# A loop over periods on five engines, written out with constant waits

## The reference

```python
h = tok(x)                        # deformable sampling: 32x32 grid of queries, 8 points each
h = concatenate([h, txt], axis=1) # 1024 + 128 = 1152 tokens of 64 channels
h = h + attention(layernorm(h))   # causal, one head, 64 wide
h = h + ffn(layernorm(h))         # 16 experts, top 2, relu, 64 -> 128 -> 64, then layer norm
```

## Time and profile before

| | us |
|---|---|
| median of 3 runs | 4752.04 |
| lowest, highest | 4744.88, 4759.59 |
| the profiled execution | 4752.51 |
| its span | 4750.7 |
| PE busy | 3648.8 (77%) |
| POOL busy | 3313.9 (70%) |
| DVE busy | 3015.8 (63%) |
| ACT busy | 2167.0 (46%) |

### The profile page before, as it was taken

The page is one execution under the profiler, slowest core; times in us unless marked ns, Lnnn a source line. Parts: engine busy times, 40 slices in busy tenths (PEclk is TensorE's granted clock), DMA queues, the critical chain, the costliest instruction groups (busy, mean ns, idle before and its releaser), DMA issues.

```text
span 4750.7 us, 94109 instructions
## 1 busy us (share of the span) xinstructions
PE 3648.8 (77%) x24896; PEld 3139.7 (66%) x24896; DVE 3015.8 (63%) x9660; ACT 2167.0 (46%) x5266; POOL 3313.9 (70%) x3217
## 2 busy tenths in 40 slices
PE   4686887878778777877878887887878788788842
PEld 2565766767667676766767676775767677676732
DVE  1485858576684857767575775858577585767512
ACT  2354554444445444444544454454454445444401
POOL 0776777777677767777677776767777776777353
PEclk9888888888889888888988888898888978888855
DMA  7759584865848477584857758485774848562422
GB/s 238 247 154 273 160 266 132 253 190 181 244 126 267 131 234 218 164 256 119 258 146 238 222 161 246 125 262 148 221 237 141 259 125 267 151 177 58 120 66 62
DMA packets 922887, 895.94 MB, mean 189 GB/s; under 512 B 123866, under 2 KB 804442, under 8 KB 922200
## 3 DMA queue, kind: packets, MB, share of 16 engines
q1 hardware_dynamic: 785800, 577.28, 40.6%
q0 software_dynamic: 136528, 312.25, 22.0%
HBM read 562.75 MB, written 328.03 MB: 188 GB/s over the span
## 4 chain that ended last, share of the span: by engine, by line
PE 26%; issue 16%; DVE 16%; POOL 16%; DMA 9%; SPq 8%; ACT 7%; DVEq 1%; ACTq 0%; POOLq 0%
POOL ya L785 7%; POOL gath L753 7%; PE ps L862 4%; DMA xg<-xs_d 3%; PE ps L1005 3%; PE ps L876 3%; PE ps L1013 3%; POOL xs_d L769 3%; PE ps L807 2%; SPq L672 2%; PE ps L937 2%; SPq L699 2%; SPq L706 2%; DMA fm<-in_x 2%; SPq L700 1%
## 5 line engine op out<-in xcount | busy, mean ns | idle before, releaser
L753 POOL DMA_INDIRECT gath<-table,idx x2048 | 2107.0, 1029 | 885.9 <-issue 625.9
L785 POOL DMA_INDIRECT ya<-ys_d,row x576 | 585.5, 1017 | 343.5 <-issue 170.3
L1215 DVE TENSOR_TENSOR prod<-gath,corner_w 128x1024 f32<-128x1024 f32 x512 | 622.7, 1220 | 313.9 <-PE ps L862 186.9
L862 PE MATMUL ps<-const,prod 128*128 128x128 f32 x4096 | 628.3, 304 | 229.8 <-DVE prod L1215 211.8
L769 POOL DMA_INDIRECT xs_d<-xm,row x576 | 611.8, 1062 | 189.3 <-issue 173.2
L862 PEld LDWEIGHTS ps<-const,prod 128*128 128x128 f32 x4096 | 541.6, 159 | 265.9 <-issue 174.3
L876 PE MATMUL ps<-w_kv,samp_t 128*128 128x128 f32 x4096 | 634.4, 305 | 7.4 <-ACT kv_sb L1029 6.7
L876 PEld LDWEIGHTS ps<-w_kv,samp_t 128*128 128x128 f32 x4096 | 588.6, 219 | 68.5 <-issue 52.6
L959 PEld LDWEIGHTS ps<-v_sb,probs_t 128*128 128x128 f32 x2880 | 402.4, 212 | 165.7 <-DVE h L1223 75.8
L959 PE MATMUL ps<-v_sb,probs_t 128*128 128x64 f32 x2880 | 423.1, 293 | 112.6 <-DVE h L1223 69.5
L1029 ACT ACTIVATE rows<-ps 128x512 f32<-128x512 f32 x512 | 305.2, 596 | 428.5 <-PE ps L807 424.9
(11 more groups left out here) (162 smaller groups left out, 6156.4 us busy)
## 6 DMA issues: line engine op xcount, KB each, us to landing
table<-rows SPq DMA_DIRECT2D x224, 1024.0 KB
fm<-in_x SPq DMA_DIRECT2D x256, 512.0 KB
wx<-w_d SPq DMA_DIRECT2D x832, 128.0 KB
gath<-table,idx POOLq DMA_INDIRECT x2048
table<-rows SPq DMA_DIRECT2D x32, 960.0 KB
xg<-xs_d SPq DMA_DIRECT2D x208, 130.0 KB
ys_d<-yx SPq DMA_DIRECT2D x208, 128.0 KB
xs_d<-xm,row POOLq DMA_INDIRECT x576
```

Source lines behind the costliest of these rows:

```text
L753: pool.indirect_dma_start(out=gath[:, n % NG, p, :], out_offset=None, in_=tables[par], in_offset=bass.IndirectOffsetOnAxis(ap=idx[:, par, ...
L785: pool.indirect_dma_start(out=ya[:, k, t, :], out_offset=None, in_=ys_d[par], in_offset=bass.IndirectOffsetOnAxis(ap=row[:, par, n:n + 1], ...
L862: last = pe.matmul(bank(0, p * P, p * P + P), prod[h][:, (p * 2 + dx) * P:(p * 2 + dx + 1) * P], ident, is_transpose=True, start=(dx == 0) ...
L1215: return dve.tensor_tensor(o, a, b, op)
```

## The change

`Pair` loses the loop's variable and is always a plain number; `drive` writes periods 0 to 14 one after the other; `settle` waits for a constant. Nothing in TURNS or LAST changes, and no tile, DMA or operation is added, moved or dropped. The counters that kept DVE's steps in line with the loop go.

```diff
-    def __init__(self, off, eng=None, turn=None):
-        self.off, self.eng, self.turn, self.products = off, eng, turn, {}
+    def __init__(self, off):
+        self.off = off
...
     def times(self, per, k=0):
 
-        if self.turn is None:
-            return self.off * per + k
-        if per not in self.products:
-            self.products[per] = self.eng.snap(self.turn * (2 * per))
-        return self.products[per] + (self.off * per + k)
+        return self.off * per + k
...
-            for k in range(LOOP_FROM):
+            for k in range(PAIRS - 1):
                 stretch(1 + k, None)
                 follow(engine, stages, k, Pair(k), k % 2)
-            with eng.Fori(0, (LOOP_TO - LOOP_FROM) // 2) as j:
-                for par in range(2):
-                    pair = Pair(LOOP_FROM + par, eng, j)
-                    stretch(LOOP, pair)
-                    follow(engine, stages, LOOP_FROM + par, pair, par)
-            for k in range(LOOP_TO, PAIRS - 1):
-                stretch(LOOP + 1 + k - LOOP_TO, None)
-                follow(engine, stages, k, Pair(k), k % 2)
-            stretch(LOOP + PAIRS - LOOP_TO, None)
+            stretch(PAIRS, None)
             follow_last(engine, stages)
...
             def settle():
 
-                n = marks.get(thread[0], start[0])
-                if before[0] is None:
-                    dve.wait_ge(vec, n)
-                else:
-                    pair, head = before[0]
-                    dve.wait_ge(vec, pair.times(STEPS[LOOP], head + n))
+                dve.wait_ge(vec, marks.get(thread[0], start[0]))
```

More of the change, by code:

```diff
@@ L231 @@
 FIRST_PART = 3
-LOOP_FROM, LOOP_TO = 2, PAIRS - 2
-LOOP = 1 + LOOP_FROM
 TURNS = {
@@ L324 @@
 class Pair:
-    def __init__(self, off, eng=None, turn=None):
-        self.off, self.eng, self.turn, self.products = off, eng, turn, {}
+    def __init__(self, off):
+        self.off = off
     def __add__(self, n):
-        p = Pair(self.off + n, self.eng, self.turn)
-        p.products = self.products
-        return p
+        return Pair(self.off + n)
     def __sub__(self, n):
@@ L580, in drive @@
                     stages[stage](Pair(0), 0, *args)
-            for k in range(LOOP_FROM):
+            for k in range(PAIRS - 1):
                 stretch(1 + k, None)
                 follow(engine, stages, k, Pair(k), k % 2)
-            with eng.Fori(0, (LOOP_TO - LOOP_FROM) // 2) as j:
-                for par in range(2):
-                    pair = Pair(LOOP_FROM + par, eng, j)
-                    stretch(LOOP, pair)
-                    follow(engine, stages, LOOP_FROM + par, pair, par)
-            for k in range(LOOP_TO, PAIRS - 1):
-                stretch(LOOP + 1 + k - LOOP_TO, None)
-                follow(engine, stages, k, Pair(k), k % 2)
-            stretch(LOOP + PAIRS - LOOP_TO, None)
+            stretch(PAIRS, None)
             follow_last(engine, stages)
-            stretch(LOOP + 1 + PAIRS - LOOP_TO, None)
+            stretch(PAIRS + 1, None)
         def first_of(pair):
-            return pair.turn is None and pair.off == 0
+            return pair.off == 0
         def begun(pair):
-            return pair.turn is not None or pair.off >= 0
+            return pair.off >= 0
         def unseen(n, pair):
@@ L1177, in _ @@
             marks = {}
-            before = [None]
             def step(ins):
@@ L1636, in _ @@
                    const[:, GY:GY + QT_N].unsqueeze(2).to_broadcast([P, QT_N, 2 * NP_]), ALU.add))
-            done = [None, 0]
             def stretch(n, pair):
-                last, count = done
                 assert not any(g.begun for g in staged), [g.begun for g in staged if g.begun]
[L1645 to L1655, removed]
                 start[0] = steps[0]
                 marks.clear()
-            setup_steps = steps[0]
             drive(dve, "vector", {"off_hidden": parts(off_hidden), "off_gelu": parts(off_gelu), "off_points": parts(off_points),
@@ L1666, in _ @@
                         "finish": parts(finish)}, stretch)
-STEPS = (34, 242, 334, 404, 404, 602)
 def kernel(**inputs):
```

## The result

The changed kernel takes 4708.69 us (median of six runs, 4705.71 to 4721.56), the kernel before 4755.82 us (six runs, 4744.88 to 4770.92). The ratio is 0.9905, with a 95% interval of 0.9889 to 0.9921: the change wins 45 us, 38 to 53. I had forecast 10. A second comparison, in another batch of runs, gave 0.9877 (0.9858 to 0.9896), 59 us of 4763.18.

The account below looks back on a forecast made before the run. POOL's queue was taken as the bound; 4752.5 us less 10 for five jumps at 2 us, with register waits and longer code at 0, gave 4742.5 us, eight-in-ten range 4708 to 4772.

Parts of the forecast that it names:

- The likeliest case: Whole kernel: little or no gain, 4738 to 4762 us; chance 0.53.
- the first two rivals: Jumps in full or more, 4715 to 4738 us, chance 0.24; register instructions count, 4650 to 4715 us, chance 0.11.
- The limit of 133 us: POOL's two stalls over the loop's twelve periods sum to 133 us, 2.8% of the span: the most quicker control can return.
- Step 2: Period 14, behind the loop with constant waits, stalls 13.5 us and takes 282.0 us against 279.0: no register saving shows.
- the slower rival: Each loop period costs what period 14 costs, 282.0 us in place of 279.0: 36 us more, 4788 us; chance 0.10.
- Step 3: The loop's five taken jumps back go: 2 us each, 10 us gained, bounds 2 and 20.
- Step 1: Register instructions ahead of the loop's waits become constants: 46 ns each on DVE, 37 ns on PE, booked at nothing.
- the second rival: Register instructions lie in the chain from period boundary to POOL's stall: 83 us gained, 4670 us; chance 0.11.
- Step 4: The five instruction streams grow to twelve written periods and fetch straight on: booked at 0.
- POOL's own 268 us a period: POOL's DMAs and gaps in each loop period, about 268 us, were taken to keep their length.
- the sign against part 3: Even and odd periods becoming alike would show the booking of 2 us a jump wrong.
- the sign against part 1: Stalls behind DVE's product below 5 us throughout would show register instructions, booked at nothing, were on the path.

Follow-up runs that it names:

- four jumps gone: Kernel before with six periods a loop turn on all engines, register waits kept, one taken jump in place of five: 4742.28 us, ratio 0.9953.
- DVE alone loops: All engines written out with constants except DVE, which keeps the kernel before's loop of six turns and register instructions: 4733.73 us, ratio 0.9942.

## Why the prediction was right in part and too small

The time, 4708.69 us, lies inside the range (4708 to 4772) by 0.7 us, and the second comparison's 4705.98 lies outside it. That it counts as inside is luck: the forecast was 4742.5. The likeliest case, little or no gain, was wrong; what happened lies between the first two rivals, by the causes of both.

**What bounds the kernel** was right: POOL with its gaps of 0.30 us, unchanged, and stalls behind DVE's product and the experts' results. What wasn't right is that transfers, and not an engine's instruction rate, set the end of the chain in front of the long stall: both stalls of a period together are 2.7 us shorter, while SP's table writes are as long as before. The limit of 133 us for the loop's periods holds, and prologue and tail are as before: from period 14's first fetch to the first one of period 17 4635.60 - 3982.97 = 652.6 us, before 4681.97 - 4030.34 = 651.6. From the timelines of POOL, changed kernel and kernel before:

```profile
4635.60 0.94 POOL L769 DMA_INDIRECT ya<-ys_d,row  x1 [42.76 <-DMA ys_d<-yx]
```

```profile
4681.97 0.94 POOL L785 DMA_INDIRECT ya<-ys_d,row  x1 [42.77 <-DMA ys_d<-yx]
```

**Step 2, period 14 as the changed kernel in miniature, failed**, and with it the likeliest case and the slower rival. Its two stalls summed to 13.5 us in before; in four other profiles, with the same orders and the same constants, they sum to 14.5 (after), 9.8 (after, second batch), 13.2 (four jumps gone), and 5.7 (DVE alone loops). The changed kernel's own constant periods 3 to 13 run from 5.1 to 11.8, in the second batch from 4.3 to 16.4. One sample of something that scatters by 9 us or more can't carry a difference of 3. I named that weakness and went by the row all the same. What I should have set against it were the means: five even and six odd periods, whose difference of 4.9 us is larger than a mean's scatter.

**Step 3, the jumps at 2 us each, was too small by a factor of two or more.** The window of 10.1 against 6.3 us on PE was real: after, it is 1128.94 - 1122.57 = 6.4 us, and no branch lies between:

```profile
1122.57 1.46 PE L997 MATMUL ps<-wx,hx 128*128 128x64 f32 x8 [0.69 <-ACT hx L1144]
1125.31 1.09 PE L981 MATMUL ps<-const,xg 128*65 128x128 f32 x4 [1.27 <-DVE yx L1193]
...
1128.94 1.91 PE L846 MATMUL ps<-const,prod 128*128 128x128 f32 x8
```

Two things were wrong. I argued from PE's branch, while DVE's jump (68 ns in the branch, 4.04 us in front of the next product) is the one on the path. And I let the distance from branch to POOL's stall in period 4 and in period 14 decide how much arrives (2.3 us at the long stall, nothing at the first fetch): again the one period. From PE's last expert product to POOL's first fetch it is 110.2 us on average over the five periods behind a jump, and 105.2 over the same periods of the changed kernel: all of the jump arrives. "Most of a jump is lost again in SP's queue" isn't what the runs show either: the pair of table writes takes 6.6 us on average in these periods, before and after. A jump costs 4 us or more: 19.3 us of DVE's idle time for five, 22 us (14 to 31) measured for four. The Trainium skill's rule that I weighed there ("Runtime: NRT & Kernel Launch", section "Instruction fetch mechanics": a taken branch out of the prefetched pages stalls for a fetch) would have had me book all five in full, 20 us; the runs of the ordinary batches side with it, while in the slower ones jumps were worth nothing (0.9983 to 1.0029 with three of five gone).

**Step 1, register waits at nothing, was wrong by some 19 to 32 us**, more than the jumps' whole booking. The reading of the earlier trace rows holds for DVE, whose chain is no closer together without them, and DVE alone with registers has the odd pairs at 274.9 against 274.6. I carried it over to the other engines, though the second rival had the reason in it: PE, ACT and SP have such instructions between the short links of the chain in front of POOL's stall, and some of them carry a wait themselves, so that nothing runs meanwhile that hides them. That this is the way in which they cost time is argued from the order of the instructions, not shown. The kernel in which DVE alone loops executes 85700 instructions, so 8409 fewer are left on the other four (11028 register instructions against 2913 plain waits); 19 to 32 us are 2 to 4 ns for each, of the 37 ns that one takes on PE: most are hidden, a small share isn't. Which of these four engines holds that share, no run in an ordinary batch tells; nor does any tell the time of the instructions from that of fetching them. Nor is DVE quite cleared: its loop cost 28 us, and five jumps at 4 to 5 us are 20 to 25 of them.

**Step 4, longer code at 0, was right**: the written-out program fetches 1.3 MB less, and nothing in front of or behind the loop's periods moved.

**POOL's own 268 us a period** weren't quite fixed, and I had said that the ground would go if they weren't. They shrink by 1.3 to 2.0 us a period, a third to half of the gain. In before, 68% of POOL's DMAs of over 1.1 us overlap one of DVE's multiplies of gathered rows, and 16% of the shorter ones; in after 73% and 16%. From the timelines of POOL and DVE, kernel before:

```profile
1875.62 1.21 DVE L1215 TENSOR_TENSOR prod<-gath,corner_w 128x1024 f32<-128x1024 f32 x1
...
1879.32 1.23 DVE L1215 TENSOR_TENSOR prod<-gath,corner_w 128x1024 f32<-128x1024 f32 x1
```

```profile
1875.85 1.81 POOL L785 DMA_INDIRECT ya<-ys_d,row  x1 [0.30 <-issue]
...
1879.39 1.98 POOL L753 DMA_INDIRECT gath<-table,idx  x1 [0.30 <-issue]
1881.67 0.95 POOL L753 DMA_INDIRECT gath<-table,idx  x1 [0.30 <-issue]
```

A DMA that starts in the first 0.3 us of such a multiply takes 1.82 us (median of 99 in before), one that starts in its last 0.3 us 0.95, and between them the time falls. How many are hit depends on where the two streams fall against each other, and the change can shift that. That the multiply is the cause is read off the coincidence; no run took it away.

**The sum as it should have been:** five jumps at 4 to 5 us, 20 to 25, and 19 to 32 for the register instructions, together 39 to 57 us; the span fell by 4750.7 - 4703.9 = 46.8, and in the second batch 59 us (50 to 68) were measured. These terms come from the same runs, so that they fit is no test of them.

**The signs I had named.** Gaps as before: yes. Register instructions and PE's 4 us gone: yes. Stalls of 10 to 14 us a period: no, 8.5 and 9.4. SP's table pairs of even periods longer than before: no, 6.6 us in both. Even and odd periods alike, the sign against part 3: nearly (9.5 and 7.7, in the second batch 9.7 and 9.1). Stalls below 5 us throughout, the sign against part 1: no; part 1 fell by a smaller amount than that sign could catch.

## What to carry to other kernels

Before you price a loop's jump, look at every engine for an idle time called "issue" in front of the first operation of a turn, times the number of turns: the branch's own row can be 68 ns and the jump 4 us, and the one on the path may be another engine's. A cost for which the profile has a regular difference over many periods (9.0 against 13.9 us, six against five) isn't refuted by one period of other code. An instruction that hides in one engine's dependent chain needn't hide in the hand-offs between engines. Adding instructions to price them works only if they leave the other waits where they were: look in the trace at which wait each one carries.

## What the hardware showed that I had not expected

- A jump costs DVE about 4 us (3.4 to 4.3 in the idle time ahead of its next product) while its branch row shows 68 ns; on PE the same time stands in the branch's own row (median 3923 ns).
- A wait for DVE's step before costs 0.10 us a step when it stands in an instruction of its own (0.91 against 0.61 us for three steps), where the register instruction of 46 ns ahead of each step had cost nothing. 13152 instructions added in this way made 133 us, while the gaps of the bounding engine stayed as they were.
- An indirect DMA on POOL takes 0.95 us alone and 1.82 us (median) where it starts in the first 0.3 us of a multiply of two SBUF operands on DVE. The Trainium skill's page "SBUF — State Buffer", section "SBUF: two separate sides", has DVE and GpSimd share a port pair that one of them holds for a whole instruction; the rows agree with such a lock, though they don't show the port.
- The same program takes 4755 us in some batches of runs and 7250 us in others, with nearly the same transfer time in the queue of images and weights (1929 and 1981 us), and the record has the same chip number for a batch of either kind. An edit can be worth 22 us in the one and nothing in the other, so a ratio is good only for the condition in which it was measured.
